# Routed gate and up products of a macaron block (MoE, time mixing, MoE): tokens stationary instead of weights, gated values turned back by transposes

## The chip, the cores and the metric

The kernel runs on one core of one Trainium2 chip. The metric is device time in microseconds, the median over runs; below it stands beside the profile of one execution.

## What is computed

The input x is 16 sequences of 512 tokens with 256 channels, f32. Three residual steps follow each other:

```python
x = x + 0.5 * ffn(layernorm(x))        # "A"
x = x + attn(layernorm(x))             # time mixing, k/v/r products, scan, layernorm, out product
x = x + 0.5 * ffn(layernorm(x))        # "B", same weights as A

def ffn(x):                            # H = 256, I = 128, 8 experts, 2 chosen per token
    shared = (silu(x @ ws_gate.T) * (x @ ws_up.T)) @ ws_down.T      # 256 inner channels
    scores = sigmoid(x @ gate_weight.T); w, idx = top_k(scores, 2); w = 2.5 * w / w.sum()
    y[e] = (silu(x @ w_gate[e].T) * (x @ w_up[e].T)) @ w_down[e].T  # 128 inner channels
    return shared + sum(w[k] * y[idx[k]])
```

## The kernel before

**Stages.** For each feed-forward ("A", then "B") the sequences are taken in four groups each (`SIZES`, L36). For a sequence: LayerNorm; the rows are split into a high and a low f16 half (`row_hi`, `row_lo`), turned by DMA into `xt` (channels on partitions, tokens along); shared products from `xt`; a router; the rank of every token within its expert; and a scatter of the rows by indirect DMA (POOL) into a DRAM buffer `xs` ordered by expert. For a group: a table says which expert each block of 128 slots belongs to. `fetch` (L737) brings blocks of `xs` by a transposing DMA into `xq`, four blocks at a time, a *quad*; the routed products run over quads; results go to DRAM (`y_store`), from where POOL gathers two rows for each token and DVE adds them (`combine`). Between A and B stands the time mixing of the sequence.

**Routed products before.** `gate_up` (L877, part "E" from L900): the table's values are loaded into registers of TensorE (L904) and the addresses of the block's weights are worked out ahead (L911). For the gate (b = 0) and then the up (b = 1) half, for each block j of the quad and each k of two halves of the channels there are three f16 products of 128 x 128 x 128 (L922, L924, L926): high weights with high rows, high weights with low rows, low weights with high rows. The weights are the stationary operand (read through a register address), the tokens move, so the result has inner channels on partitions and 128 tokens along: one PSUM bank holds the gate of four blocks, a second the up. ACT takes silu of the gate bank into `hid` (L1129, `silu`), DVE multiplies by the up bank (L1227, `gated`), and `hid` is at once in the right orientation to be the stationary operand of `down` (L962, f32, the expert's 128 x 256 down weights moving; one product shows as two instructions in the profile). ACT copies the two banks of `down` to `y_sb` (L1146, `evac`).

**Shared products.** L893 to L895 (512 tokens move), gating as above, then a split of `hid` (`hidden_hi`, `hidden_lo`) and f16 products of 256 columns with tokens stationary (L954, L956, L958).

**Other products.** k, v and r projections (L1029), transposes by TensorE of f32 tiles (L1019 before the mixing, L1049 after the scan), the out product (L1063), router (L976, L979).

**Order.** Every engine's instruction list is written by a planner (`Plan`, L64, and `schedule`, L233). Each task has an engine, a cost in us and an urgency; the planner runs the program in its own model and gives each engine the most urgent task that is ready and for which a buffer is free. The urgencies are sums of a due time and a lag: `LATER` by kind, `T_LATER`, `A_LATER`, `B_LATER` by sequence, `G_LATER` by group. PSUM is six banks for everything and two for `down`. `gate_up` of up to four quads may run ahead of their `down` (`AHEAD`), `hid` has four buffers, `xq` four. The engines then run their lists in order, with semaphore waits.

Of the kernel before, what the change touches and what calls it, by code (L numbers as in the profile page):

```python
# [13 lines left out]
P = 128  # L14
# [39 lines left out]
GATE_0, UP_0, GATE_1, UP_1, DOWN = range(5)  # L54
# [18 lines left out]
class Plan:  # L73
# [10 lines left out]
    SHARED = ("hidden_hi", "hidden_lo")  # L84
# [36 lines left out]
    def run(self, takes, frees, follows):  # L121
# [22 lines left out]
        while events:  # L144
# [13 lines left out]
            for e in order:  # L158
# [3 lines left out]
                for k in ready[e]:  # L162
# [3 lines left out]
                    if stream and stream[1] is not None:  # L166
# [3 lines left out]
                        if k[0] in self.SHARED:  # L170
                            n = sum(other[0] == "S" for other in list(turn[stream[0]])[:n])
                        if line.get((k[0], stream[0]), 0) != n:
                            continue
# [59 lines left out]
def schedule():  # L233
    plan = Plan()

    LATER = {"bias": -6.3, "bonus": -53.3, "choose": 17.5, "combine": 1.0, "downE": -14.8, "evac": 17.4, "fetchA": 2.5, "fetchB": 36.2, "gate_upE": 1.8, "gate_upS": 0.6, "gatedE": 8.2, "gatedS": 2.6, "gatherA": 3.5, "gatherB": -15.9, "hidden_hi": 2.6, "hidden_lo": 1.8, "k_copy": 19.6, "k_proj": -61.7, "kv": -17.5, "mix": -0.2, "norm1": -1.5, "norm2": -60.6, "norm3": 50.1, "out_proj": 0.1, "out_resid": -15.2, "part": -65.4, "places": -10.6, "r_proj": -18.8, "rank": -8.4, "receive": -16.5, "resid": 18.2, "route_exp": -8.2, "router": -2.2, "row_hi": 1.3, "row_lo": -12.8, "rstd": -23.6, "rstd_o": -39.0, "scan": -16.6, "scan_turn": 1.3, "scatter": 2.1, "siluE": -15.7, "siluS": 42.3, "stats1": -8.4, "stats2": -6.8, "stats3": 10.4, "stats_o": 14.3, "store": -27.3, "table": -28.2, "table_out": 25.9, "table_turn": -23.3, "tails": -18.3, "top2": -10.7, "total": -0.9, "turn2": -4.9, "turn_rows": -21.3, "v_proj": -29.1, "weights": 0.9, "y_places": 77.9, "y_store": 15.0}
    T_LATER = (-3.2, 0.2, 12.0, -1.8, 3.6, 4.1, 2.4, 5.3, 12.6, -3.2, -4.1, -4.2, -6.1, -13.4, -5.3, -22.0)
    A_LATER = (-3.4, 0.4, -11.1, -2.1, -14.2, -14.7, -19.1, -15.8, -19.6, -17.4, -24.0, -17.7, -21.2, -21.2, -28.9, -11.5)
    B_LATER = (7.4, 15.7, -12.7, -4.0, 9.8, 4.4, 2.8, 10.9, 23.2, 48.0, 74.2, 65.5, 17.7, 54.6, 24.9, 30.2)
    G_LATER = (-3.0, -4.9, -0.1, 11.8, -23.7, 20.7, -21.9, 25.5)  # L240
# [148 lines left out]
    for g in GROUPS["B"]:  # L389
# [3 lines left out]
            "total": 1, "table_turn": 1, "o_bias": 1, "o_mean": 1, "gate_up": 2}  # L393
# [16 lines left out]
    def frees(k):  # L410
# [9 lines left out]
        if name == "silu":  # L420
            gone(("gate_up", key), "bank", 0)
        elif name == "gated":
            gone(("gate_up", key), "bank", 1)
        elif name == "mix":
# [31 lines left out]
    def follows(k):  # L456
# [8 lines left out]
        if name in ("silu", "gated", "hidden_hi", "hidden_lo", "down"):  # L465
# [8 lines left out]
def program(nc, x, w_chunks, w_attn, w_router, channels, consts_in, xs, ys, out):  # L474
# [26 lines left out]
    with ExitStack() as ctx:  # L501
# [3 lines left out]
        def sem(name):  # L505
# [6 lines left out]
        w_hi = [sb(f"w_hi{p}", [P, NCH * P], F16) for p in range(DOWN)]  # L512
        w_lo = [sb(f"w_lo{p}", [P, NCH * P], F16) for p in range(DOWN)]

        wd = sb("wd", [P, 2, NE * P])
# [14 lines left out]
        w_stage = acc[:, NSEQ // 2:, :, :].rearrange("p s j c -> p (s j c)")[:, 0:NCH * GU]\  # L530
            .rearrange("p (c u n) -> p c u n", c=NCH, u=4)
# [91 lines left out]
        silu_done, gated_done = sem("silu_done"), sem("gated_done")  # L623
        hi_done, lo_done = sem("hi_done"), sem("lo_done")
# [33 lines left out]
        def released(name, key, b):  # L658

            if name == "gate_up":  # L660
                return (silu_done, gated_done)[b], chunk_no[key] + 1
            if name == "down":
# [28 lines left out]
        def slots_of(what, f, *which):  # L691
            return T if what == "S" else blocks_of(f, *which) * P

# [10 lines left out]
        def _(sp):  # L704
# [62 lines left out]
            def load_w(i):  # L767
# [5 lines left out]
                for c in range(*SPLITS[i]):  # L773
                    sp.dma_start(w_stage[:, c].rearrange("p u n -> p (u n)"), w_chunks[c][:, 0:GU]).then_inc(w_in[i], 16)
                    to = wd[:, :, c * P:(c + 1) * P] if c < NE else ws_stage[:, :, (c - NE) * P:(c - NE + 1) * P]
                    sp.dma_start(to, w_chunks[c][:, GU:CW].rearrange("p (h n) -> p h n", h=2)).then_inc(wd_in[i], 16)
# [93 lines left out]
        def _(pe):  # L870
# [9 lines left out]
            def gate_up(what, f, *which):  # L880
                key = (what, f, *which)
                if what == "S":
# [5 lines left out]
                    cols = slice((NE + c) * P, (NE + c + 1) * P)  # L888
                    for b, done in ((0, gate_done), (1, up_done)):
                        bank = bank_free("gate_up", key, b)  # L890
# [681 lines left out]
```

## Time and profile before

| | us |
|---|---|
| median of 3 runs | 1129.08 (1127.78 to 1136.01) |
| span of the profiled execution | 1279.5 |
| what lies around the span | not recorded; no separate time of that execution was kept |
| PE busy in the profiled execution | 991.1 (77%) |
| DVE, POOL, ACT busy | 788.2, 695.5, 412.1 |

The profiled execution's span is 150 us longer than the median of the plain runs. Busy times of PE are modelled and overlap, so the spacing of matmuls is read from their starts. PE is the matmuls, PEld the weight loads, PEldq and PEq TensorE's sequencer, L12 a line of the kernel.

### The profile page before, as it was taken

Reading aid. Unit: us, or ns where it says so; the run is one execution under the profiler, and the core shown is the slowest. Engines: PE = TensorE matmul, PEld = TensorE weight load, DVE = VectorE, ACT = ScalarE, POOL = GpSimd, SP = SyncE. Lnnn points to the kernel's source line nnn. Section 1 sums busy time; section 2 is a strip of 40 time slices with the busy share of each in tenths; the row PEclk is TensorE's granted clock in tenths of the full one; section 3 lists DMA queues with packets and bytes.
Section 4 is the critical chain, followed back from the end, with each engine's and each line's share of the span. In section 5 each row is a group of like instructions: output and inputs, shape, how many; then the busy total and the mean of one; then the engine's idle time right before and its main releaser. Section 6 shows DMA issues by size and latency. Waiting matters only on the chain.

```text
span 1279.5 us, 23262 instructions
## 1 busy us (share of the span) xinstructions
PE 991.1 (77%) x7488; PEld 696.8 (54%) x7488; DVE 788.2 (62%) x2485; ACT 412.1 (32%) x737; POOL 695.5 (54%) x684
## 2 busy tenths in 40 slices
PE   2767986889957876989867899778787997877560
PEld 1434663565835544657755576456465675656450
DVE  5855554979655875875247697554587885324233
ACT  5332441445313532423213354112233533212110
POOL 2766445764156885274256334754667455355555
PEclk9888988999979887999878899888988999878875
DMA  8668689673266632337777535764876346679974
GB/s 241 203 182 165 131 217 201 141 177 105 66 150 140 152 99 87 79 103 188 170 166 179 132 83 106 175 188 134 208 154 164 94 92 185 163 184 246 225 194 139
DMA packets 337989, 198.58 MB, mean 155 GB/s; under 512 B 251728, under 2 KB 319952, under 8 KB 337872
## 3 DMA queue, kind: packets, MB, share of 16 engines
q1 hardware_dynamic: 312432, 129.84, 41.8%
q0 software_dynamic: 24576, 67.14, 20.6%
q8 instruction: 64, 1.05, 0.4%
q14 instruction: 53, 0.43, 0.1%
q10 hardware_dynamic: 864, 0.12, 0.1%
HBM read 47.05 MB, written 92.27 MB: 109 GB/s over the span
## 4 chain that ended last, share of the span: by engine, by line
PE 51%; issue 18%; DVE 11%; another core or an unknown queue 7%; POOL 6%; DMA 3%; ACT 2%; SPq 1%; ACTq 0%; POOLq 0%; DVEq 0%
PE ps L1029 11%; PE ps L962 10%; PE ps L922 5%; PE ps L924 5%; PE ps L926 5%; PE ps L1063 3%; PE ps L895 2%; PE ps L893 2%; PE ps L894 2%; POOL xsB L835 2%; DVE acc L1254 2%; PE ps L954 1%; POOL y_got L852 1%; PE ps L958 1%
## 5 line engine op out<-in xcount | busy, mean ns | idle before, releaser
L922 PE MATMUL ps<-xq,w_hi 128*128 128x128 f16 x1248 | 238.2, 231 | 45.2 <-issue 37.8
L926 PE MATMUL ps<-xq,w_lo 128*128 128x128 f16 x1248 | 239.1, 231 | 35.7 <-issue 35.6
L924 PE MATMUL ps<-xq,w_hi 128*128 128x128 f16 x1248 | 238.9, 231 | 29.5 <-issue 29.2
L1227 DVE SCALAR_TENSOR_TENSOR hid<-ps,hid 128x512 f32<-128x512 f32 x144 | 97.2, 678 | 220.2 <-remote 112.3
L962 PE MATMUL ps<-wd,hid 128*128 x624 | 175.1, 425 | 33.2 <-ACT y_sb L1146 11.2
L1129 ACT ACTIVATE hid<-ps 128x512 f32<-128x512 f32 x144 | 85.1, 591 | 328.1 <-remote 185.2
L852 POOL DMA_INDIRECT y_got<-ysB,y_pos x128 | 124.9, 975 | 99.3 <-DVE acc L1254 50.4
L835 POOL DMA_INDIRECT xsB<-rows,pos x128 | 131.6, 1028 | 79.3 <-DVE pos L1384 43.1
L835 POOL DMA_INDIRECT xsA<-rows,pos x128 | 132.1, 1032 | 74.2 <-DVE pos L1384 38.8
L1254 DVE SCALAR_TENSOR_TENSOR acc<-y_got,share,acc 128x256 f32<-128x256 f32 x256 | 127.8, 507 | 58.3 <-DMA y_got<-ysB,y_pos 31.2
L962 PEld LDWEIGHTS ps<-wd,hid 128*128 128x128 f32 x624 | 128.0, 213 | 65.4 <-issue 47.2
L922 PEld LDWEIGHTS ps<-xq,w_hi 128*128 x1248 | 129.2, 104 | 57.8 <-issue 50.4
L852 POOL DMA_INDIRECT y_got<-ysA,y_pos x128 | 130.1, 1016 | 51.1 <-issue 35.8
L924 PEld LDWEIGHTS ps<-xq,w_hi 128*128 x1248 | 129.3, 104 | 43.6 <-issue 40.1
L926 PEld LDWEIGHTS ps<-xq,w_lo 128*128 x1248 | 129.6, 104 | 40.9 <-issue 40.7
L1146 ACT COPY y_sb<-ps 128x512 f32<-128x512 f32 (+1 forms) x160 | 84.2, 581 | 177.6 <-PE ps L962 122.4
L809 POOL TENSOR_TENSOR rstd<-var_eps,neg_half 128x4 f32<-128x4 f32 x48 | 52.2, 1088 | 109.9 <-DVE less_mean L1278 93.4
L893 PE MATMUL ps<-xt,w_hi 128*128 128x512 f16 x256 | 102.9, 402 | 11.1 <-ACT hid L1129 6.2
L895 PE MATMUL ps<-xt,w_lo 128*128 128x512 f16 x256 | 102.3, 400 | 1.9 <-issue 1.9
L894 PE MATMUL ps<-xt,w_hi 128*128 128x512 f16 x256 | 102.6, 401 | 0.3 <-issue 0.2
L826 POOL TENSOR_TENSOR p_exp<-inv_e,best 128x8 f32<-128x8 f32 x32 | 53.9, 1686 | 83.3 <-DVE best L1319 80.6
L954 PE MATMUL ps<-ws_hi,hid_h 128*128 128x256 f16 x256 | 75.0, 293 | 28.5 <-DVE hid_l L1234 19.9
(138 smaller groups left out, 1804.4 us busy)
## 6 DMA issues: line engine op xcount, KB each, us to landing
ysA<-y_sb SPq DMA_DIRECT2D x36, 512.0 KB
ysB<-y_sb SPq DMA_DIRECT2D x36, 512.0 KB
acc<-in_x_dram SPq DMA_DIRECT2D x16, 512.0 KB
out_dram<-acc SPq DMA_DIRECT2D x16, 512.0 KB
xsA<-zeros SPq DMA_DIRECT2D x36, 128.0 KB
xsB<-zeros SPq DMA_DIRECT2D x36, 128.0 KB
acc<-in_w_chunks_dram SPq DMA_DIRECT2D x10, 256.0 KB, 4.7
xq<-xsA SPq DMA_TRANSPOSE x156
```

The lines of the kernel that those rows point to most:

```text
L835: g.indirect_dma_start(out=xs[f, group_of(f, s)], out_offset=bass.IndirectOffsetOnAxis(ap=pos[:, n % N_ROWS, j, k:k + 1], axis=0), in_=row ...
L852: g.indirect_dma_start(out=y_got[:, h, k, :], out_offset=None, in_=ys[f, g_no], in_offset=bass.IndirectOffsetOnAxis(ap=y_pos[:, s, h, k:k ...
L893: nc.tensor.matmul(ps[:, bank, :], w_hi[2 * k + b][:, cols], hi, start=(k == 0), stop=False)
L894: nc.tensor.matmul(ps[:, bank, :], w_hi[2 * k + b][:, cols], lo, start=False, stop=False)
L895: mm = nc.tensor.matmul(ps[:, bank, :], w_lo[2 * k + b][:, cols], hi, start=False, stop=(k == KC - 1))
L922: nc.tensor.matmul(half, w_hi[2 * k + b][:, cols], hi, start=(j == 0 and k == 0), stop=False, skip_group_check=True)
L924: nc.tensor.matmul(half, w_hi[2 * k + b][:, cols], lo, start=False, stop=False, skip_group_check=True)
L926: mm = nc.tensor.matmul(half, w_lo[2 * k + b][:, cols], hi, start=False, stop=(j == many - 1 and k == KC - 1), skip_group_check=True)
L962: mm = nc.tensor.matmul(half, hid[:, b, tok], wd[:, :, cols], start=(j % 2 == 0), stop=(j % 2 == 1 or j == many - 1), skip_group_check=True)
L1029: mm = nc.tensor.matmul(ps[:, bank, :], a32[:, "kvr".index(w), k, m * P:(m + 1) * P], mixed[w][:, k, :], start=(k == 0), stop=(k == KC - 1))
L1227: v.scalar_tensor_tensor(out=hid[:, i % N_HID, some], in0=ps[:, bank_of("gate_up", key, 1), some], scalar=W_UNSCALE, in1=hid[:, i % N_HID, ...
L1254: v.scalar_tensor_tensor(out=acc[:, s, h, :], in0=y_got[:, h, k, :], scalar=share[:, s, h, k:k + 1], in1=acc[:, s, h, :], op0=ALU.mult, op ...
```

## The change

In the routed part the tokens become the stationary operand and the weights move. The weights of gate and up of one expert lie side by side (256 columns, `GU2`), so one product yields gate and up of a block: tokens on partitions, 256 columns along. A block takes 6 products of 256 columns instead of 12 of 128. Bank 0 now holds gate and up of the quad's first two blocks, bank 1 those of the other two. `silu` and `gated` work on each bank by itself. The result has tokens on partitions, so it is turned back: `turn` (four f32 transposes on TensorE into one more PSUM bank) and `unturn` (an ACT copy from it into `hid`), before `down`. The down weights of an expert lie in one run. The shared products keep their form; only where their weights lie changes. The table holds the expert's number times 256 instead of 128. All lags and due times of the planner are new: every value of `LATER`, `T_LATER`, `A_LATER`, `B_LATER` and `G_LATER`, and those that stand in the diff.

```diff
-    FIRST_A = 6.9
-    FIRST_T = 111.2
-    A_LEAD = 243.5
+    FIRST_A = 5.5
+    FIRST_T = 111.1
+    A_LEAD = 243.2
...
-    E_LEAD = 33.4
-    B_LAG = 73.4
-    EB_LAG = 59.1
+    E_LEAD = 32.9
+    B_LAG = 74.1
+    EB_LAG = 63.3
...
-    G_LAG = 84.0
+    G_LAG = 63.8
...
-        add("pe", "gate_up", key, 0.725 * blocks_of(f, a, b) if what == "E" else 2.75, at, after)
-        add("act", "silu", key, 0.6, at + 1.5, [("gate_up", key)])
-        add("dve", "gated", key, 0.7, at + 2, [("silu", key)])
+        add("pe", "gate_up", key, 0.66 * blocks_of(f, a, b) if what == "E" else 2.75, at, after)
+        add("act", "silu", key, 0.6 if what == "S" else 0.8, at + 1.5, [("gate_up", key)])
+        add("dve", "gated", key, 0.7 if what == "S" else 0.9, at + 2, [("silu", key)])
...
-            add("pe", "down", key, 0.48 * blocks_of(f, a, b), at + 4, [("gated", key)])
+            add("pe", "turn", key, 0.132 * blocks_of(f, a, b), at + 3, [("gated", key)])
+            add("act", "unturn", key, 0.63, at + 3.5, [("turn", key)])
+            add("pe", "down", key, 0.48 * blocks_of(f, a, b), at + 4, [("unturn", key)])
...
                 for j in range(many):
-                    for p in range(DOWN):
+                    for k in range(KC):
                         for w in (w_hi, w_lo):
-                            nc.tensor.lower_ap(w[p][:, bass.ds(first[j], P)], for_matmul_weights=True)
+                            nc.tensor.lower_ap(w[k][:, bass.ds(first[j], GU2)])
...
-                    for j in range(many):
-                        half = ps[:, bank, j * P:(j + 1) * P]
-                        cols = bass.ds(first[j], P)
+                    for j in range(2 * b, min(2 * b + 2, many)):
+                        both = ps[:, bank, (j % 2) * GU2:(j % 2 + 1) * GU2]
+                        cols, tok = bass.ds(first[j], GU2), slice(j * P, (j + 1) * P)
                         for k in range(KC):
-                            hi = xq[:, n % N_XQ, k, j * P:(j + 1) * P]
-                            lo = xq[:, n % N_XQ, KC + k, j * P:(j + 1) * P]
-                            nc.tensor.matmul(half, w_hi[2 * k + b][:, cols], hi, start=(j == 0 and k == 0),
+                            hi, lo = xq[:, n % N_XQ, k, tok], xq[:, n % N_XQ, KC + k, tok]
+                            nc.tensor.matmul(both, hi, w_hi[k][:, cols], start=(j % 2 == 0 and k == 0),
                                              stop=False, skip_group_check=True)
-                            nc.tensor.matmul(half, w_hi[2 * k + b][:, cols], lo, start=False, stop=False,
+                            nc.tensor.matmul(both, hi, w_lo[k][:, cols], start=False, stop=False,
                                              skip_group_check=True)
-                            mm = nc.tensor.matmul(half, w_lo[2 * k + b][:, cols], hi, start=False,
-                                                  stop=(j == many - 1 and k == KC - 1), skip_group_check=True)
+                            mm = nc.tensor.matmul(both, lo, w_hi[k][:, cols], start=False,
+                                                  stop=(k == KC - 1 and j in (2 * b + 1, many - 1)),
+                                                  skip_group_check=True)
                     mm.then_inc(done, 1)
+
+            def turn(*key):
+                i, many = chunk_no[key], blocks_of(*key[1:])
+                pe.wait_ge(gated_done, i + 1)
+                bank = bank_free("turn", key, 0)
+                for j in range(many):
+                    tok = slice(j * P, (j + 1) * P)
+                    mm = nc.tensor.transpose(ps[:, bank, tok], hid[:, i % N_HID, tok], ident[:])
+                mm.then_inc(hid_turned, 1)
...
-                        cols = bass.ds(expert_cols[key][j], P)
-                        mm = nc.tensor.matmul(half, hid[:, b, tok], wd[:, :, cols], start=(j % 2 == 0),
+                        half = ps[:, out[j // 2], (j % 2) * C:(j % 2 + 1) * C]
+                        cols = bass.ds(expert_cols[key][j], C)
+                        mm = nc.tensor.matmul(half, hid[:, b, tok], wd[:, cols], start=(j % 2 == 0),
                                               stop=(j % 2 == 1 or j == many - 1), skip_group_check=True)
...
+                for b, (ready, done) in enumerate(((gate_done, silu_first), (up_done, silu_done))):
+                    act.wait_ge(ready, i + 1)
+                    gate, some = quad_half(key, b, 0)
+                    nc.scalar.activation(some, gate, ACT.Silu, scale=W_UNSCALE).then_inc(done, 1)
+
+            def unturn(*key):
+                i, some = chunk_no[key], slice(0, slots_of(*key))
+                act.wait_ge(hid_turned, quad_no[key[1:]] + 1)
+                nc.scalar.copy(hid[:, i % N_HID, some], ps[:, bank_of("turn", key, 0), some]).then_inc(unturned, 1)
...
+                for b, (ready, n, done) in enumerate(((silu_first, quad_no[key[1:]], gated_first),
+                                                      (silu_done, i, gated_done))):
+                    dve.wait_ge((gate_done, up_done)[b], i + 1)
+                    dve.wait_ge(ready, n + 1)
+                    up, some = quad_half(key, b, 1)
+                    v.scalar_tensor_tensor(out=some, in0=up, scalar=W_UNSCALE, in1=some, op0=ALU.mult,
+                                           op1=ALU.mult).then_inc(done, 1)
```

`quad_half` picks, of bank b, the gate (side 0) or up (side 1) columns of its two blocks, and the place in `hid` for them. Both `gate_up` banks of a quad are given back by `gated`, the bank of `turn` by `unturn`.

## Rows read from the trace of the kernel before

**Rows 1.** The page: busy us (share) x instructions; granted clock in 40 slices.
```profile
span 1279.5 us, 23262 instructions
...
PE 991.1 (77%) x7488; PEld 696.8 (54%) x7488; DVE 788.2 (62%) x2485; ACT 412.1 (32%) x737; POOL 695.5 (54%) x684
...
PEclk9888988999979887999878899888988999878875
```

**Rows 2.** The page: the chain that ended last, by engine.
```profile
PE 51%; issue 18%; DVE 11%; another core or an unknown queue 7%; POOL 6%; DMA 3%; ACT 2%; SPq 1%; ACTq 0%; POOLq 0%; DVEq 0%
```

**Rows 3.** Windows: start:end, length, busy PE PEld DVE ACT POOL, clock, DMA, GB/s.
```profile
100.00:1080.00 980.00, 818.23 (x6045) 572.15 (x6044) 656.87 (x2045) 339.27 (x605) 542.71 (x518) 0.91 0.60 143
...
1080.00:1280.00 200.00, 117.75 (x1052) 93.82 (x1049) 63.24 (x157) 32.41 (x61) 97.56 (x102) 0.78 0.74 191
```

**Rows 4.** TensorE's waits: us in total, times, longest us.
```profile
PE ps L922 <- issue: 37.8, 58, 2.7
...
PE ps L926 <- issue: 35.6, 41, 1.9
...
PE ps L924 <- issue: 29.2, 38, 3.3
...
PE ps L962 <- DVE hid L1227: 10.8, 2, 8.7
...
PE ps L954 <- issue: 8.4, 7, 3.1
...
PE ps L958 <- issue: 2.5, 3, 1.1
...
PE ps L956 <- issue: 1.8, 3, 1.1
```

**Rows 5.** The chain in order of time: start us, us, what.
```profile
291.54 1.73 PE ps L962 x8
...
640.01 0.06 PE ps L924
...
643.29 3.29 issue
...
656.06 0.11 PE ps L922
```

**Rows 6.** The timeline: start us, us, engine, line, operation, count.
```profile
619.84 0.27 PE L954 MATMUL ps<-ws_hi,hid_h 128*128 128x256 f16 x1
...
621.04 0.27 PE L958 MATMUL ps<-ws_lo,hid_h 128*128 128x256 f16 x1
...
621.15 0.22 PE L922 MATMUL ps<-xq,w_hi 128*128 128x128 f16 x1
...
623.77 0.22 PE L926 MATMUL ps<-xq,w_lo 128*128 128x128 f16 x1
...
999.98 1.04 PE L1049 MATMUL ps<-ident,state 128*128 128x128 f32 x8
```

**Rows 7.** Three single lines: duration ns min/median/max.
```profile
L904 PEldq TENSOR_LOAD <-tabA x40: 327/334/2647, 90.9 to 887.5; - x40
...
L1049 PE MATMUL ps<-ident,state x128: 269/273/421, 260.8 to 1049.4; 128*128 128x128 f32 x128
...
L911 PEldq FUSED_REGOPS  x472: 51/74/84, 91.5 to 1234.6; - x158
```

**Rows 8.** Groups by shape: busy us, mean ns | idle before, releasers.
```profile
L922 PEld LDWEIGHTS ps<-xq,w_hi 128*128 x1248 | 129.2, 104 | 57.8 <-issue 50.4 <-DMA xq<-xsB 5.2
...
L1227 DVE SCALAR_TENSOR_TENSOR hid<-ps,hid 128x512 f32<-128x512 f32 x136 | 92.8, 686 | 206.8 <-remote 106.7 <-ACT hid L1129 43.1 <-PE ps L926 41.7
...
L1129 ACT ACTIVATE hid<-ps 128x512 f32<-128x512 f32 x136 | 81.1, 597 | 309.9 <-remote 185.2 <-PE ps L926 55.8 <-PE ps L895 50.1
...
L1489 DVE SCALAR_TENSOR_TENSOR acc<-ps,rstdo,acc 128x256 f32<-128x256 f32 x64 | 26.6, 476 | 7.6 <-PE ps L1063 4.4 <-POOL rstdo L819 3.2
...
L1146 ACT COPY y_sb<-ps 128x256 f32<-128x256 f32 x8 | 3.0, 378 | 0.0
```

More of the change, by code:

```diff
@@ L51 @@
 AHEAD = 4
-GATE_0, UP_0, GATE_1, UP_1, DOWN = range(5)
+GU2 = 2 * P
 SPLITS = ((NE, NCH), (0, 4), (4, NE))
@@ L82 @@
     WINDOW, FULL, BESIDE = 3.413, 0.75, 0.9
-    SHARED = ("hidden_hi", "hidden_lo")
+    SHARED, ROUTED = ("hidden_hi", "hidden_lo"), ("turn", "unturn")
     RINGS = ("xt", "xq", "rows", "hid", "split", "y")
@@ L171, in run @@
                             n = sum(other[0] == "S" for other in list(turn[stream[0]])[:n])
+                        if k[0] in self.ROUTED:
+                            n = sum(other[0] == "E" for other in list(turn[stream[0]])[:n])
                         if line.get((k[0], stream[0]), 0) != n:
@@ L392, in schedule @@
     uses = {"turn2": 2, "k_proj": 1, "v_proj": 1, "r_proj": 1, "scan_turn": 2, "out_proj": 2, "router": 1, "rank": 1,
[L393 removed]
+            "total": 1, "table_turn": 1, "o_bias": 1, "o_mean": 1, "gate_up": 2, "turn": 1}
     def takes(k):
@@ L420, in frees @@
         if name == "silu":
-            gone(("gate_up", key), "bank", 0)
+            if key[0] == "S":
+                gone(("gate_up", key), "bank", 0)
         elif name == "gated":
+            if key[0] == "E":
+                gone(("gate_up", key), "bank", 0)
             gone(("gate_up", key), "bank", 1)
+        elif name == "unturn":
+            gone(("turn", key), "bank", 0)
         elif name == "mix":
@@ L464, in follows @@
             return "chunks", None, key
-        if name in ("silu", "gated", "hidden_hi", "hidden_lo", "down"):
+        if name in ("silu", "gated", "hidden_hi", "hidden_lo", "turn", "unturn", "down"):
             return "chunks", key
@@ L508, in program @@
         ps = ctx.enter_context(nc.psum_tensor("ps", [P, 8, 512], F32))
-        w_hi = [sb(f"w_hi{p}", [P, NCH * P], F16) for p in range(DOWN)]
-        w_lo = [sb(f"w_lo{p}", [P, NCH * P], F16) for p in range(DOWN)]
-        wd = sb("wd", [P, 2, NE * P])
+        w_hi = [sb(f"w_hi{k}", [P, NCH * GU2], F16) for k in range(KC)]
+        w_lo = [sb(f"w_lo{k}", [P, NCH * GU2], F16) for k in range(KC)]
+        wd = sb("wd", [P, NE * C])
         ws_hi = sb("ws_hi", [P, 2, NSH * P], F16)
@@ L660, in released @@
             if name == "gate_up":
+                if key[0] == "E" and b == 0:
+                    return gated_first, quad_no[key[1:]] + 1
                 return (silu_done, gated_done)[b], chunk_no[key] + 1
+            if name == "turn":
+                return unturned, quad_no[key[1:]] + 1
             if name == "down":
@@ L692, in slots_of, with quad_half @@
             return T if what == "S" else blocks_of(f, *which) * P
+        def quad_half(key, b, side):
+            many = min(2, blocks_of(*key[1:]) - 2 * b)
+            bank, i = bank_of("gate_up", key, b), chunk_no[key]
+            side_by_side = ps[:, bank, 0:many * GU2].rearrange("p (j u n) -> p j u n", j=many, u=2)
+            return (side_by_side[:, :, side, :],
+                    hid[:, i % N_HID, 2 * b * P:(2 * b + many) * P].rearrange("p (j n) -> p j n", j=many))
         def uses(n, buf, of):
@@ L936, in down @@
                 else:
-                    pe.wait_ge(gated_done, i + 1)
+                    pe.wait_ge(unturned, quad_no[(f, *which)] + 1)
                 if what == "E" and which[1] == 0:
@@ L1085, in _ @@
             pe.wait_ge(consts_dma, 16 * 5)
-            do = {"gate_up": gate_up, "down": down, "router": router, "rank": rank, "total": total,
+            do = {"gate_up": gate_up, "turn": turn, "down": down, "router": router, "rank": rank, "total": total,
                   "table_turn": table_turn, "turn2": turn2, "k_proj": k_proj, "v_proj": v_proj, "r_proj": r_proj,
@@ L1108, in split_hi @@
                     act.wait_ge(w_in[i - 1], 16 * (last - first))
-                    for p in range(DOWN):
-                        ins = nc.scalar.activation(w_hi[p][:, first * P:last * P].rearrange("p (c n) -> p c n", n=P),
-                                                   w_stage[:, first:last, p], ACT.Copy, scale=W_SCALE)
+                    for k in range(KC):
+                        ins = nc.scalar.activation(w_hi[k][:, first * GU2:last * GU2]
+                                                   .rearrange("p (c n) -> p c n", n=GU2),
+                                                   w_stage[:, first:last, k], ACT.Copy, scale=W_SCALE)
                     if i == 1:
@@ L1213, in split_lo @@
                     first, last = SPLITS[i - 1]
-                    cols = slice(first * P, last * P)
-                    for p in range(DOWN):
-                        ins = low(w_lo[p][:, cols].rearrange("p (c n) -> p c n", n=P), w_stage[:, first:last, p],
-                                  w_hi[p][:, cols].rearrange("p (c n) -> p c n", n=P))
+                    cols = slice(first * GU2, last * GU2)
+                    for k in range(KC):
+                        ins = low(w_lo[k][:, cols].rearrange("p (c n) -> p c n", n=GU2), w_stage[:, first:last, k],
+                                  w_hi[k][:, cols].rearrange("p (c n) -> p c n", n=GU2))
                     if i == 1:
```

59 lines of the change are left out of this document (33 added, 26 removed).

## Prediction

> **What bounds the kernel now.** I read the page's busy table and slices first, then the chain that ended last, then the windows, then TensorE's waits, and last the single instructions of one quad. The reader is to see five things.
>
> TensorE has the most work: 991.1 us of a span of 1279.5, with the granted clock mostly near full [rows 1]. The chain that ended last is PE for 51% and "issue" for 18%, then DVE for 11%; ACT has 2% [rows 2]. So about 69% of the path is TensorE working, or standing with nothing to wait for.
>
> The kernel has two stretches. From 100 to 1080 us PE is busy 818 of 980 us; in the last 200 us it is busy 118, at a mean clock of 0.78 and a DMA share of 0.74 [rows 3]. There it is not TensorE's work that sets the pace.
>
> TensorE's own longest waits are "issue" ahead of the three routed gate and up products: 37.8 + 35.6 + 29.2 = 102.6 us over 3744 matmuls, 27 ns each. The same kind of wait ahead of the shared down products of 256 columns (L956, L958) is 1.8 + 2.5 us over 512 matmuls, 8 ns each [rows 4]. They come in bursts: where a matmul takes 0.06 us on the chain at 640.01, a piece of issue of 3.29 us stands a few matmuls later in the same quad [rows 5].
>
> The span is 150 us longer than the median of the runs, 1129.08. The chain's issue is 18% of 1279.5, about 228 us. Recording is the only thing known to differ between the two, and waits that scale with the number of recorded instructions are the first candidate. If the 150 us all came out of issue, 78 of 228 would be left, a third (0.34). I use this as the upper share of an issue wait that a plain run also has, and zero as the lower one. Terms of the sum are read at the profiled execution's scale; where they are array time they go onto the median unchanged, where they are issue they are scaled by that share.
>
> **Routed products.** There are 312 blocks of 128 slots (3744 / 12) in 80 quads (40 of A at L904 [rows 7], as many of B). Before, a block costs 12 matmuls of 128 columns. Between the first L922 of the quad at 621.15 and its last L926 at 623.77 there are 47 steps, 55.7 ns each: 0.669 us a block. After, it is 6 matmuls of 256 columns of the same type. The nearest rows are the shared down products: L954 at 619.84 to L958 at 621.04 is 11 steps, 109.1 ns each [rows 6]: 0.655 us. The same columns pass through the array, so only the small cost per matmul is saved: 0.014 x 312 = 4 us. At the low clock level a 128-column step is 0.11 us [rows 5], twice the columns' time at the full level, and there the form gives back nothing. Bounds: 0 and 4 us; I take 4.
>
> The Trainium skill (TensorE: Matmul & The Clock Gate, Back-to-back issue gap) says that in a stream of weight-load and matmul pairs the sustained spacing at 128 columns is about 81 ns, and that the plain column formula counts too little there. By that a block would cost 0.97 us now and the change would be worth about 0.32 x 312 = 99 us of array time, an estimate from that page. The trace disagrees: the pairs here stand 55.7 ns apart with a fresh weight load for each, so the sum goes by the rows; what would follow if loads did bind is a rival below.
>
> **Transposes.** 312 are added, f32, 128 x 128. The kernel has the same form at L1049: eight take 1.04 us and one lasts 0.273, so a step is (1.04 - 0.27) / 7 = 0.110 us [rows 6, 7]. 312 x 0.110 = 34 us at the full level. The mean granted clock of 0.91 in the middle [rows 3] means that some stretches are at the low level (1.2 instead of 2.4 GHz), where a step is twice as long: with one transpose in seven there, an estimate from that mean less its idle part, 39 us. Bounds 34 and 68. The down product keeps its operands' sizes, 1.73 us for eight instructions of four blocks [rows 5]; its weights now lie in one run instead of two pieces; cost 0, bounds -2 and +2. The addresses worked out per block fall from eight to four; that group of PE's register operations is 472 x 74 ns = 35 us of its sequencer [rows 7], mostly behind matmuls already issued; I give it 0, bounds -10 and 0.
>
> Array time: 39 - 4 = +35 us. As 69% of the chain is PE and issue, I put 0.69 x 35 = 24 us on the path; the ends are 0 and 35.
>
> **Issue waits.** At the 8 ns of 256-column products, 1872 of them cost 16 us. Counting L954's 8.4 us too [rows 4], it is 12.7 / 768 = 17 ns and 31 us. Between them 24, and 3 for the transposes (at L1049 2.6 us for 128): 102.6 - 27 = 76 us less in a profiled execution. On the median I take half of the upper share: 0.17 x 76 = 13 us less; the ends are 0 and 76. The upper end is the case that issue is all real.
>
> **Gating in halves.** Each PSUM bank now holds gate and up of two blocks, so silu and gating are two instructions each. ACT: a 128x256 copy out of PSUM takes 378 ns, the 128x512 silu 597, so +0.16 us a quad; and the new copy of the turned values, which has the silu's size, 0.59: +0.75 x 80 = 60 us of ACT. DVE: a 128x256 operation out of PSUM takes 476 ns, the 128x512 gating 686 [rows 8]: +0.27 x 80 = 21 us. ACT has 2% of the chain and DVE 11% [rows 2]: 1 and 2 us. What hides ACT's 60 is its 32% load [rows 1]; without that cover they cost up to 60.
>
> **The chain of a quad.** Before, after the last up product only the gating (0.69) stands before down. After: silu of the second half 0.38, gating 0.48, four transposes 0.44, copy 0.59: 1.89, so 1.2 us later, plus two more semaphore hops. In the middle other quads and sequences fill that (up to four quads run ahead). It is bare at the end of the last groups: 2 us, bounds 0 and 10. A new wait stands in PE's queue twice: ahead of turn (gated values) and of down (the copy); whatever the new order has put behind them waits too, since one engine's waits are met in the order of its queue. The existing form of this wait, L962 on DVE, is 10.8 us [rows 4]. The turn also takes one of six banks for about 1.1 us a quad, 88 of 6 x 1129 bank-microseconds, 1%: nothing.
>
> **Orders.** All lags are new, and with them SP's and POOL's queues. No instruction of either is added or dropped, and the DMAs have the same sizes (the down weights load as 1 KB runs instead of two of 512 B, once). I give this 0, bounds -15 and +15: no row shows an order that was not run.
>
> **Sum.** 24 - 13 + 2 + 1 + 2 = +16; I round down to +15, as part of the 24 is bound to fall into other engines' waits: 1129 + 15 = 1144 us. For a profiled execution 24 + 5 - 0.69 x 76 = -23: a span near 1256, shorter than before although the plain run is longer.
>
> **Rivals.**
> Issue is real (faster). The bursts of issue [rows 5] hit dense 128-column streams, whatever is recorded, and the change halves their number. For it: the waits per instruction fall from 27 to 8 ns with the wider form [rows 4]. Against it: 150 us of span that plain runs don't have. Price: all of it 24 + 5 - 76 = -47, 1082; a half, -9, 1120. It decides from 29 us of real saving, 38% of the 76, onwards. Chance 0.27, at about 1108.
>
> Loads bind (faster). If a pair held the array for the 104 ns of its weight load [rows 8], a block would take 1.25 us now and 0.655 after, 186 us of array and 0.69 of it on the path: 1129 - 128 + 29 = 1030. The spacing of 55.7 ns speaks against it [rows 6]. Chance 0.02. This is where the rule of 81 ns would lead.
>
> Hidden (no change). PE is idle 162 of the middle's 980 us [rows 3]; if the new order puts turns there, the 35 us cost a third: 1129 + 12 - 13 + 3 = 1131. Chance 0.22.
>
> Waits in order (slower). If half of the 1.2 us longer chain is bare in each quad, 80 x 0.6 = 48 us and 0.69 of it on the path, 33: 1144 + 33 = 1177. For it: one DVE wait at L962 lasted 8.7 us of the 10.8; against it: there were only two. Chance 0.14.
>
> **How the numbers follow.** The forecast has 0.35, with its own range 1132 to 1158 (array on the path 15 to 30, issue 0 to 26, order a few). A measurement of this kernel tells about 1% from no change, 11 us. Faster by over 1% (under 1118): most of the rival with real issue and the 0.02, 0.25. Within 1%: the hidden case, the rest of the first rival and a part of the forecast, 0.32. Slower by over 1% (over 1140): 0.43. Range: 1098 to 1172, which leaves out the ends of the two outer rivals.
>
> **What would show it.** Right: the gate and up group reads x1872 at 256 columns, spaced 0.109; x312 transposes at 0.11; issue ahead of gate and up falls from 103 to 20 to 35 us; span 1235 to 1275. Wrong: a median under 1118 with the span falling by as much as the median (issue was real); L962 or the transposes waiting over 30 us for ACT or DVE (waits in order); gate and up spaced other than 0.109; PE busy outside 100 to 1080 us grown instead of inside.

## The result and the profile after

The changed kernel takes 1158.5 us (median of 4, 1157.4 to 1159.6) against 1131.8 for the kernel before (1127.8 to 1136.0): ratio 1.023, 95% interval 1.020 to 1.027. It is slower, as forecast, by 27 us where +15 was forecast.

The page of the changed kernel: span, busy times, granted clock, and the chain by engine.
```profile
span 1157.4 us, 20370 instructions
...
PE 955.8 (83%) x5928; PEld 667.1 (58%) x5928; DVE 809.1 (70%) x2559; ACT 462.2 (40%) x891; POOL 700.3 (61%) x684
...
PEclk9989999999999989999899999899889999988985
...
POOL 20%; PE 19%; issue 18%; SPq 16%; DVE 12%; DMA 11%; ACT 2%; POOLq 0%; ACTq 0%; DVEq 0%
```
The first surprise is the span: 1157.4, two microseconds from the plain time. The profile read before the prediction was 1279.5, 150 over its plain time, and [rows 1, 2] came from it. So the kernel before was profiled once more, unchanged:

> The kernel before, profiled once more. Theory R (the waits called issue were the recording's): the profiled execution can be anywhere from 1130 to 1280 us, its plain time is 1130, ratio 1.00, and where its span is near 1130 the issue waits ahead of the routed gate and up products are under 15 us instead of 103. Rival (issue is the kernel's own): the span is near 1280 again with about 100 us of issue.

Plain 1132.1 (10 runs), ratio 0.999 (0.997 to 1.002), span of the profiled execution 1130.8. Its page:
```profile
span 1130.8 us, 23262 instructions
...
PE 921.7 (82%) x7488; PEld 667.1 (59%) x7488; DVE 800.4 (71%) x2485; ACT 410.5 (36%) x737; POOL 697.3 (62%) x684
...
PEclk9889999999999989999899899989999999989885
...
PE 23%; POOL 22%; issue 18%; SPq 12%; DVE 11%; DMA 11%; ACT 2%; POOLq 0%; ACTq 0%; DVEq 0%
```
Its waits of TensorE that end in issue, all that the view's first 30 rows have, beside 102.6 us for three lines in [rows 4]:
```profile
PE ps L922 <- issue: 9.8, 15, 1.3
...
PE ps L954 <- issue: 4.2, 3, 2.1
...
PE ps L1063 <- issue: 2.4, 1, 2.4
```
Two things change for the reader. The bursts of [rows 5] belong to the one execution in which they were recorded. And the chain is another one: PE holds 23% of it, not 51%; POOL, SP's queue and DMA hold 45%. The 51% stood on an execution in which TensorE was busy 69 us longer and idle 79 us longer than in the second (991.1 of 1279.5 us against 921.7 of 1130.8); that this made it the late one is my reading. Why that execution was so long is not shown: the second was recorded too. From here on every comparison of profiles is made against this second profile of the kernel before.

What the change does to single instructions is as the prediction had it. The changed kernel's timeline, one quad:
```profile
708.56 0.27 PE L947 MATMUL ps<-w_hi,xq 128*128 x1
...
711.07 0.27 PE L951 MATMUL ps<-w_hi,xq 128*128 x1
```
23 steps in 2.51 us, 109.1 ns each, 0.655 us a block (0.655 predicted). The new transposes, and the halves of silu and gating and the new copy, by line and by group:
```profile
L962 PE MATMUL ps<-ident,hid x312: 272/273/477, 100.4 to 1118.6; 128*128 128x128 f32 x156
```
```profile
L1172 ACT ACTIVATE hid<-ps 128x256 f32<-128x256 f32 x152 | 55.9, 383 | 155.8 <-PE ps L951 147.4 <-PE ps L998 4.3 <-issue 3.1
...
L1283 DVE SCALAR_TENSOR_TENSOR hid<-ps,hid 128x256 f32<-128x256 f32 x152 | 59.1, 418 | 54.1 <-ACT hid L1172 53.9
...
L1177 ACT COPY hid<-ps 128x512 f32<-128x512 f32 x72 | 41.9, 587 | 91.5 <-PE ps L962 81.8 <-issue 9.4
```
383 ns (378 taken), 418 ns (476 taken), 587 ns (590 taken). PE's busy time rises from 921.7 to 955.8, by 34 us; PE's time not busy falls only from 209 to 202 (span less busy). That leaves the question: why was the added work not done in the time in which PE stands? Windows of the kernel before (second profile), then of the changed kernel; columns as in [rows 3]:
```profile
100.00:1000.00 900.00, 796.18 (x6391) 574.00 (x6388) 672.13 (x2054) 344.79 (x619) 554.18 (x531) 0.97 0.69 162
1000.00:1131.00 131.00, 65.14 (x662) 56.76 (x662) 54.20 (x119) 21.56 (x40) 82.22 (x85) 0.79 0.90 237
```
```profile
100.00:1000.00 900.00, 803.28 (x4931) 559.19 (x4928) 674.48 (x2107) 380.47 (x737) 546.70 (x520) 0.97 0.66 157
1000.00:1157.00 157.00, 90.70 (x584) 72.34 (x584) 59.66 (x140) 37.56 (x80) 92.39 (x95) 0.82 0.90 225
```
In the 900 us of the middle PE is busy 7 us longer, and 26 us more of its work is left for the end, which is 26 us longer. Yet 97 us of the middle stay idle. Either the form needs that idle time (its longer chain and its two waits), or the new order does. One sign was on hand before any run: each kernel's planner computes the length of the whole program in its own model (below, the planner's length), and it gives 1068.5 us for the kernel before and 1091.2 for the changed one, 23 us more.

### The profile page after: what moved, and what is told of

Same layout as the page of the kernel before. It is cut to its first block, busy times and chain, and to the rows that moved or that the text cites. A ratio compares the mean times of both kernels' runs of the same rounds, so it can differ in the third digit from the quotient of the medians.

```text
span 1157.4 us, 20370 instructions
## 1 busy us (share of the span) xinstructions
PE 955.8 (83%) x5928; PEld 667.1 (58%) x5928; DVE 809.1 (70%) x2559; ACT 462.2 (40%) x891; POOL 700.3 (61%) x684
## 4 chain that ended last, share of the span: by engine, by line
POOL 20%; PE 19%; issue 18%; SPq 16%; DVE 12%; DMA 11%; ACT 2%; POOLq 0%; ACTq 0%; DVEq 0%
SPq L775 10%; PE ps L1065 6%; POOL y_got L878 6%; POOL xsA L861 5%; DMA y_got<-ysB,y_pos 4%; POOL xsB L861 4%; PE ps L998 3%; DVE acc L1309 2%; PE ps L1099 2%; SPq L748 2%; DMA xq<-xsB 2%; PE ps L947 2%; POOL rstd L835 2%; DMA y_got<-ysA,y_pos 2%; PE ps L949 1%
## 5 line engine op out<-in xcount | busy, mean ns | idle before, releaser
L1309 DVE SCALAR_TENSOR_TENSOR acc<-y_got,share,acc 128x256 f32<-128x256 f32 x256 | 133.5, 523 | 127.2 <-DMA y_got<-ysB,y_pos 75.0
L947 PE MATMUL ps<-w_hi,xq 128*128 x624 | 180.4, 289 | 49.3 <-DMA xq<-xsB 31.3
L949 PE MATMUL ps<-w_lo,xq 128*128 x624 | 180.5, 289 | 0.0
L951 PE MATMUL ps<-w_hi,xq 128*128 x624 | 180.1, 289 | 0.0
L861 POOL DMA_INDIRECT xsA<-rows,pos x128 | 135.2, 1057 | 61.5 <-issue 35.4
L998 PE MATMUL ps<-wd,hid 128*128 x624 | 151.2, 385 | 14.5 <-ACT hid L1177 7.0
L998 PEld LDWEIGHTS ps<-wd,hid 128*128 128x128 f32 x624 | 114.3, 192 | 34.0 <-issue 19.5
L1172 ACT ACTIVATE hid<-ps 128x256 f32<-128x256 f32 (+1 forms) x160 | 58.0, 378 | 157.7 <-PE ps L951 149.2
L947 PEld LDWEIGHTS ps<-w_hi,xq 128*128 128x128 f16 x624 | 64.4, 103 | 71.0 <-DMA xq<-xsB 35.0
L1283 DVE SCALAR_TENSOR_TENSOR hid<-ps,hid 128x256 f32<-128x256 f32 (+1 forms) x160 | 61.0, 411 | 54.9 <-ACT hid L1172 54.6
L1204 ACT ACTIVATE norm<-acc,shift,rstd 128x256 f32<-128x256 f32 x128 | 66.4, 591 | 65.1 <-POOL shift L838 52.0
L1177 ACT COPY hid<-ps 128x512 f32<-128x512 f32 x80 | 45.5, 578 | 92.4 <-PE ps L962 82.7
```

Source lines behind the costliest of these rows:

```text
L861: g.indirect_dma_start(out=xs[f, group_of(f, s)], out_offset=bass.IndirectOffsetOnAxis(ap=pos[:, n % N_ROWS, j, k:k + 1], axis=0), in_=row ...
L947: nc.tensor.matmul(both, hi, w_hi[k][:, cols], start=(j % 2 == 0 and k == 0), stop=False, skip_group_check=True)
L949: nc.tensor.matmul(both, hi, w_lo[k][:, cols], start=False, stop=False, skip_group_check=True)
L951: mm = nc.tensor.matmul(both, lo, w_hi[k][:, cols], start=False, stop=(k == KC - 1 and j in (2 * b + 1, many - 1)), skip_group_check=True)
L998: mm = nc.tensor.matmul(half, hid[:, b, tok], wd[:, cols], start=(j % 2 == 0), stop=(j % 2 == 1 or j == many - 1), skip_group_check=True)
L1309: v.scalar_tensor_tensor(out=acc[:, s, h, :], in0=y_got[:, h, k, :], scalar=share[:, s, h, k:k + 1], in1=acc[:, s, h, :], op0=ALU.mult, op ...
```

## The experiments

All ratios are to the kernel before, measured on the same chip.

**Which half of the change?** The changed kernel under the lags of before:
```diff
-    EB_LAG = 63.3
-    G_LAG = 63.8
+    EB_LAG = 59.1
+    G_LAG = 84.0
...
```


> The changed kernel with the lags and due times of before. Theory A (the added TensorE work is the loss): 1150 to 1185 us, not below the changed kernel's 1158.5. Rival O (the new lags are the loss): 1125 to 1140 us.

1179.5 us, ratio 1.041 (1.036 to 1.047). And the other way round, the old form under the new lags (the same lines exchanged in the kernel before):

> The kernel before with the lags and due times of the changed one. Theory A: the lags were fitted to the other form, so 1130 to 1170 us, no better than before. Rival O (the new lags are bad in themselves): 1155 us or more, as slow as the changed kernel.

1162.2 us, ratio 1.028 (1.023 to 1.033). A's ranges hold for both runs. O's range for the first (1125 to 1140) is missed by 40 us, but its bound for the second holds: a kernel with none of the added work that is as slow as the change. Exchanging lags is no clean cut, because lags fitted to one set of costs are unfitted to another: both mixtures are slower than their own form with its own lags.

**Taking the added work out, order kept.** In the changed kernel:
```diff
             def turn(*key):
-                i, many = chunk_no[key], blocks_of(*key[1:])
-                pe.wait_ge(gated_done, i + 1)
...
+                pass
...
             def unturn(*key):
...
+                pass
...
-                    pe.wait_ge(unturned, quad_no[(f, *which)] + 1)
+                    pe.wait_ge(gated_done, i + 1)
```


> The changed kernel without the transposes and without the copy behind them, order unchanged; down reads the values unturned, so the routed output is another one. Theory A (transposes and copy are the loss, 39 us of array of which most is on the path): 1120 to 1135 us. Rival H (gating in halves and the 256-column products are the loss): above 1150 us.

1148.9 us, ratio 1.018 (1.011 to 1.024): between the ranges of A and H, 14 us above A's. Without the transposes, the copy and their two waits 10 of the 27 us come back by the medians and 6 by the ratios, and the intervals of the two ratios overlap, so it could be nothing. The kernel that is left is busy on TensorE for as long as the kernel before (923.2 and 921.7 us on their pages) and is still 16 us slower than it was on the same chip (1133.2). What it has besides is the halves, the 256-column products, their banks (the first one is now held until its half is gated) and the order.

Where the work was taken out TensorE stands instead, ahead of the routed products and mostly for fetched rows. First the changed kernel, then this one:
```profile
L947 PE MATMUL ps<-w_hi,xq 128*128 x624 | 180.4, 289 | 49.3 <-DMA xq<-xsB 31.3
```
```profile
L946 PE MATMUL ps<-w_hi,xq 128*128 x624 | 181.2, 290 | 78.1 <-DMA xq<-xsB 47.8
```
It waits 29 us longer there, where 33 us of TensorE's busy time are gone.

**Doubling.** The changed kernel with every transpose twice:
```diff
-                for j in range(many):
+                for j in [*range(many), *range(many)]:
                     tok = slice(j * P, (j + 1) * P)
                     mm = nc.tensor.transpose(ps[:, bank, tok], hid[:, i % N_HID, tok], ident[:])
```


> The changed kernel with every transpose made twice, the same order: 312 more at 0.110 us, 34 us of array. Theory P (TensorE's array time goes to the span one for one): 1158.5 + 30 to 38 = 1188 to 1197 us. Rival C (what costs is the longer chain with its two waits, which grows only by 0.44 us a quad, mostly covered): 1160 to 1172 us.

1159.4 us, ratio 1.025 (1.019 to 1.030); the change has 1.023. This is the run that fells theory P, on which my sum rested: 34 us more of array (27 us more of busy time on the page) cost 1 to 2 us, with an interval of about 6 us either way. Its windows show where they went:
```profile
100.00:1000.00 900.00, 823.68 (x5166) 583.81 (x5165) 672.71 (x2104) 381.79 (x735) 545.31 (x519) 0.97 0.67 157
1000.00:1160.00 160.00, 96.59 (x655) 78.76 (x652) 60.21 (x142) 38.30 (x82) 93.11 (x96) 0.85 0.89 222
```
PE is busy 824 us of the middle instead of 803: the doubled transposes stand in time that was idle in the same order.

The copy twice, one after the other:
```diff
+                nc.scalar.copy(hid[:, i % N_HID, some], ps[:, bank_of("turn", key, 0), some]).then_inc(copied, 1)
+                act.wait_ge(copied, quad_no[key[1:]] + 1)
                 nc.scalar.copy(hid[:, i % N_HID, some], ps[:, bank_of("turn", key, 0), some]).then_inc(unturned, 1)
```


> The changed kernel with ACT's copy of the turned values made twice, one after the other: the chain of a quad grows by about 0.7 us and ACT by 50 us, TensorE by nothing. Theory P: 1158 to 1166 us. Rival C: half or more of 80 x 0.7 = 56 us, 1185 us or more.

1160.1 us, ratio 1.026 (1.022 to 1.031): +2 to 3 us against the change, inside P's range. The chain of a quad, longer by a second copy of 0.59 us and the wait between the two, is covered in this order. Rival C (1185 us or more) falls too.

**Single parts in the kernel before.** Silu and gating of a quad in two halves:
```diff
-                some = slice(0, slots_of(*key))
-                nc.scalar.activation(hid[:, i % N_HID, some], ps[:, bank_of("gate_up", key, 0), some], ACT.Silu,
-                                     scale=W_UNSCALE).then_inc(silu_done, 1)
+                for some in halves(key):
+                    ins = nc.scalar.activation(hid[:, i % N_HID, some], ps[:, bank_of("gate_up", key, 0), some],
+                                               ACT.Silu, scale=W_UNSCALE)
+                ins.then_inc(silu_done, 1)
...
```


> The kernel before, its order, with the silu and the gating of a quad as two instructions of half the width each: ACT +13 us, DVE +21 us, TensorE nothing. Theory P: 1132 to 1140 us. Rival D (the work added to DVE is a good part of the loss): 1145 us or more.

1132.5 us, ratio 1.000 (0.997 to 1.003): nothing, and rival D falls. By the pages the halves add 7 us of DVE and 5 of ACT here, not the 21 and 13 expected. And the array time of the transposes alone, in the fitted order of before:
```diff
+                if what == "E":
+                    for j in range(many):
+                        tok = slice(j * P, (j + 1) * P)
+                        nc.tensor.transpose(ps[:, out[0], tok], hid[:, b, tok], ident[:])
```


> The kernel before, its order, with four transposes of the gated values ahead of each routed down product into the bank that this product then overwrites: 34 us of array, no new wait and no copy. Theory P: 1132 + 28 to 38 = 1160 to 1170 us. Rival C (waits, not array time): 1132 to 1145 us.

1140.3 us, ratio 1.009 (1.006 to 1.012): 10 us for 34 (25 by the page's busy time), under P's range and within C's. Array time counts by 0.3 to 0.4 here. The other direction:
```diff
-                            nc.tensor.matmul(half, w_hi[2 * k + b][:, cols], lo, start=False, stop=False,
-                                             skip_group_check=True)
-                            mm = nc.tensor.matmul(half, w_lo[2 * k + b][:, cols], hi, start=False,
+                            mm = nc.tensor.matmul(half, w_hi[2 * k + b][:, cols], lo, start=False,
                                                   stop=(j == many - 1 and k == KC - 1), skip_group_check=True)
```


> The kernel before, its order, with the third of the three routed gate and up products (low weights) left out: 1248 matmuls of 55.7 ns, 69 us of array less. If array time under a fixed order counts one for one: 1062 us. If it counts by a third, as the 34 us of idle transposes did (10 us): 1105 to 1115 us. If the order's waits set all: 1125 to 1132 us.

1123.9 us, ratio 0.993 (0.990 to 0.996): 8 us for 69 (51 by the page's busy time, 921.7 to 870.5), a tenth to a sixth, outside the range for a third and 1 us below that for waits alone. Its windows:
```profile
100.00:1000.00 900.00, 762.00 (x5411) 530.51 (x5409) 678.34 (x2067) 346.07 (x623) 561.71 (x540) 0.95 0.72 165
1000.00:1118.00 118.00, 50.71 (x430) 41.91 (x430) 48.60 (x109) 19.80 (x37) 73.71 (x76) 0.76 0.88 243
```
PE is busy 34 us less in the middle than in the kernel before and simply stands 34 us more there. TensorE is busy for 82% of the span of the kernel before, and still isn't what that kernel waits for most.

**New orders.** No part of the work that was tried accounts for the loss, so the order was next. (The 256-column products and the longer-held bank were not tried by themselves.) A search over the planner's lags, the same for each kernel, gave other orders; in the kernel before, for example, and in the changed one:
```diff
-    EB_LAG = 59.1
-    G_LAG = 84.0
+    EB_LAG = 65.2
+    G_LAG = 52.7
...
-    EB_LAG = 63.3
-    G_LAG = 63.8
+    EB_LAG = 60.0
+    G_LAG = 82.9
...
```
(the other lags differ by similar amounts). The third kernel is that without transposes and copy, and here they are gone from the plan too:
```diff
-            add("pe", "turn", key, 0.132 * blocks_of(f, a, b), at + 3, [("gated", key)])
-            add("act", "unturn", key, 0.63, at + 3.5, [("turn", key)])
-            add("pe", "down", key, 0.48 * blocks_of(f, a, b), at + 4, [("unturn", key)])
+            add("pe", "down", key, 0.48 * blocks_of(f, a, b), at + 4, [("gated", key)])
```

> The kernel before with lags searched anew for it; the planner's own length falls from 1068.5 to 1052.3 (the chip was 61 to 70 us above the planner's length in the four full forms run so far). Theory F (what the order loses or gains on the chip follows the planner): 1112 to 1124 us. Rival N (the planner's gains below its tuned point are noise): 1130 us or more.

> The changed kernel with lags searched anew, as long a search starting from the lags of before; planner's length 1080.7 against 1091.2 of the change. Theory F: 1142 to 1154 us, faster than the change but 25 to 35 us slower than the old form planned again. Rival N: 1155 us or more. Rival U (only the search of the change was unlucky): within 8 us of the old form planned again.

> The new form without transposes and copy, and planned without them (planner's length 1058.8); down reads the values unturned, so the routed output is another one. Theory T (transposes and copy are the form's loss once each kernel has an order of its own): 1120 to 1132 us, 20 us or more below the new form planned again. Rival H (the rest of the form costs as much): above 1138 us.

Measured: 1131.6 us, ratio 0.999 (0.997 to 1.001); 1136.8 us, ratio 1.004 (1.001 to 1.007); 1137.9 us, ratio 1.008 (1.004 to 1.011). The new form with another order is 22 us faster than the change and within half a per cent of the kernel before. The old form gained nothing from 16 us of the planner's length. And the kernel without transposes and copy, with an order of its own, is no faster than the full one: the whole of the added work is worth less than the difference between two orders. Theory F is refuted (its first range missed by 8 us, its second by 5), theory T is missed by 6 us, and U holds for this pair of orders. N holds for the old form and fails by 18 us for the new one; H is at its edge (1137.9 against above 1138).

One order each proves little, so two more for each form were made in the same way, from other starting points. The edit is again the lags only; two of them, for the two new-form kernels and then for the two old-form ones:
```diff
-    EB_LAG = 63.3
-    G_LAG = 63.8
+    EB_LAG = 64.9
+    G_LAG = 53.7
...
+    EB_LAG = 71.5
+    G_LAG = 25.6
...
-    EB_LAG = 59.1
-    G_LAG = 84.0
+    EB_LAG = 53.7
+    G_LAG = 104.6
...
+    EB_LAG = 63.5
+    G_LAG = 32.0
```

> The changed kernel's form with a second order, searched from the lags that were found for the old form (planner's length 1087.3, 4 below that of the change). Theory O (the change's order is an unlucky one among orders that the planner holds equal): anywhere from 1135 to 1165 us. Rival U (the form costs 20 us or more): 1155 us or more.

> As the run before, a third order from another starting point (planner's length 1089.9). Theory O: 1135 to 1165 us. Rival U: 1155 us or more.

> The old form with an order searched from the lags of the new form planned again (planner's length 1061.3, 7 below that of the kernel before). Theory O: 1128 to 1160 us, overlapping the new form's orders. Rival U: 1120 to 1135 us, 20 us below them.

> As the run before, from the starting point of the third order (planner's length 1061.8). Theory O: 1128 to 1160 us. Rival U: 1120 to 1135 us.

Measured, in that order: 1172.5 us, ratio 1.036 (1.031 to 1.042), above the range of O; 1150.9, 1.018 (1.013 to 1.023); 1139.9, 1.007 (1.004 to 1.010); 1139.1, 1.006 (1.003 to 1.009). With the earlier ones:

The windows are those of one profiled execution each; that of the new form planned again took 1131.0 us, the fastest of its ten.

| full kernels | planner's length | PE busy, 100 to 1000 us | PE busy / length of the end | us | ratio |
|---|---|---|---|---|---|
| new form, planned again | 1080.7 | 823 | 64 / 130 | 1136.8 | 1.004 |
| new form, third order | 1089.9 | 815 | 84 / 150 | 1150.9 | 1.018 |
| new form, the change | 1091.2 | 803 | 91 / 157 | 1158.5 | 1.023 |
| new form, second order | 1087.3 | 792 | 102 / 169 | 1172.5 | 1.036 |
| new form, lags of before | 1109.7 | 790 | 111 / 179 | 1179.5 | 1.041 |
| old form, the kernel before | 1068.5 | 796 | 65 / 131 | 1131.8 | 1 |
| old form, planned again | 1052.3 | 800 | 70 / 131 | 1131.6 | 0.999 |
| old form, second order | 1061.3 | 798 | 69 / 139 | 1139.9 | 1.007 |
| old form, third order | 1061.8 | 801 | 70 / 137 | 1139.1 | 1.006 |
| old form, lags of the change | 1103.3 | 790 | 81 / 152 | 1162.2 | 1.028 |

The windows of the best and the worst searched order of the new form:
```profile
100.00:1000.00 900.00, 822.72 (x5102) 578.53 (x5102) 678.67 (x2123) 388.10 (x754) 548.37 (x530) 0.97 0.68 161
1000.00:1130.00 130.00, 63.80 (x400) 50.38 (x400) 52.90 (x128) 27.82 (x60) 82.71 (x85) 0.80 0.92 243
```
```profile
100.00:1000.00 900.00, 792.01 (x4843) 548.93 (x4844) 671.61 (x2103) 378.88 (x730) 535.70 (x514) 0.97 0.64 154
1000.00:1169.00 169.00, 101.97 (x660) 80.59 (x658) 63.19 (x148) 41.41 (x90) 98.48 (x102) 0.80 0.86 224
```
The reader is to see the same pattern in the five rows of the new form. In the last stretch PE stands 66 to 68 us, whatever the order (130 - 64, 150 - 84, 157 - 91, 169 - 102, 179 - 111); in the old form's it is 61 to 71. About 35 us of them lie behind the last down product, where the chain is POOL's gathers, their DMAs and DVE's adds. In the change and in the new form planned again that product is
```profile
1120.20 1.56 PE L998 MATMUL ps<-wd,hid 128*128 x6 [1.30 <-ACT hid L1177]
```
```profile
1092.29 1.56 PE L998 MATMUL ps<-wd,hid 128*128 x6 [1.30 <-ACT hid L1177]
```
and the spans are 1157.4 and 1129.2: 35.6 and 35.4 us behind its end. So the end is as long as these 66 us and the work that is left at 1000 us, and what the order decides is how much of PE's work fits into the middle. The best one does 823 us of it there, with all the added transposes; the change 803.

Does the form cost anything? Over the four searched orders of each form (the change and the kernel before among them), the ratios are 1.004, 1.018, 1.023, 1.036 and 0.999, 1.000, 1.006, 1.007: means 1.020 and 1.003, best against best half a per cent. The sets overlap at one kernel only, and the spread inside the new form, 3.2%, is larger than the change's loss, that inside the old one 0.8%. So neither theory of the last four expectations holds as it was put: the new form can be had for 6 us, but an order found for it in this way costs 19 us more on average than one for the old form, and is more of a lottery. Four orders each fix that average poorly (a standard error of 8 us). The planner's own lengths have a gap of the same kind, 1087.3 and 1061.0 on average, 26 us. They do not rank the orders: the chip is 56 to 85 us above them in these eight, and the new form's worst searched order (1172.5) has its second shortest length.

## Why the prediction was wrong, step by step

**What bounds the kernel: failed, and with it the weight of the array.** "So about 69% of the path is TensorE working, or standing with nothing to wait for" was read from an execution 150 us longer than the plain runs. In the second profile PE is 23% of the chain. From the 69% I put 24 of 35 us of array on the path. At a kept order, 34 us more of array cost 10 us in the kernel before and 1 to 2 in the changed one, and 69 us less gave 8. The term should have been between 1 and 10 us; the rival "hidden" had it about right, at a third of the array, and the sum of 1131 us wrong. A sign of this stood in the prediction as one of being wrong: of the 34 us by which PE's busy time grew, 14 lie between 100 and 1080 us and 20 outside.

**Issue waits: failed in size, the bound held.** I gave back 13 us. The bound "zero as the lower one" is where the truth lies: issue ahead of the routed gate and up products is 9.8 us in the second profile of the kernel before and 4.0 in the changed kernel's, so at most 6 were to be had. The reason given, that 150 us of the span had no counterpart in plain runs, was right; it should have taken the whole term away, and cast doubt on the chain as well. (The 3 us for the transposes were also too small by their own row: 2.6 us for 128 make 6 for 312, which changes the sum by half a microsecond.) The rival "issue is real" fell with it; so did the forecast of a span near 1256.

**Routed products, transposes, halves, copy: right in size.** 0.655 us a block as predicted, 0.273 us a transpose as at L1049, ACT 0.38 and 0.59 as taken, DVE 0.42 instead of 0.48. The 81 ns a pair that the Trainium skill (TensorE: Matmul & The Clock Gate, Back-to-back issue gap) gives for 128 columns is not what these traces show, 55.7 ns; nor do they show the 99 us of array estimated from it. Halves alone cost 0 (ratio 1.000); the forecast had 3 us for them and the copy together.

**The chain of a quad: right.** I gave 2 us. The copy made twice adds 2 to 3 us, and down waits for the new copy only 7 us in all in the changed kernel:
```profile
PE ps L962 <- DVE hid L1283: 16.6, 8, 5.0
...
PE ps L998 <- ACT hid L1177: 7.0, 7, 3.3
```
The rival "waits in order" had as its mark over 30 us of such waits. These two are 24 together, 31 with down's other waits for ACT and DVE (6.3 and 1.0 us), so the mark doesn't decide; the doubled copy does, which was covered.

**Orders: the step that failed most.** "I give this 0, bounds -15 and +15: no row shows an order that was not run." The order of the change costs 22 us against another order of the same work (1158.5 and 1136.8), outside these bounds, and 81% of the loss. That other order is the best of four; against their mean (1154.7) the change's costs 4 us, so most of what the term lacked is not one unlucky order but what this form's searched orders cost on average. The planner's lengths, 1068.5 and 1091.2, had 23 us of it and were in the two kernels when I put the term at nothing. The sign of the forecast was right by luck: a term that was too large (array) stood in for one that I had put at nothing. The kernel without the added work in the change's order, still 1.8% slower than before, is the run that shows it most directly. What makes an order a bad one isn't settled, nor why this form's are worse on average; the runs show where it costs (how much work is left for the end), not by which task, and no single lag was tried by itself.

## What to carry to other kernels

Where a profiled execution is much longer than the plain runs, take a second profile before the chain or any wait is believed. A high busy share does not make an engine's array time count one for one: doubling the suspected work in place, with the order kept, costs one run and tells what it is worth in that order. And where every list is planned, a new form and its new order are two changes: the planner's own lengths are to be read first, and several orders of each have to be compared before the form is judged.

## What the runs showed of the hardware that I had not expected

A profiled execution can be 13% longer than the plain runs of its kernel (1279.5 us of span, granted clock 0.891) and the next one of the same kernel not at all (1130.8, clock 0.941). No run shows whether the recording did it.

Transposes on TensorE did not lower the granted clock. With 34 us more of them at a kept order its mean over the plain runs was 0.943 in the old form (0.937 in the kernel before on the same chip) and 0.947 in the new one (0.939 in the change), steps hardly larger than the spread between executions of one kernel (0.930 to 0.943 in that kernel before). With 69 us of products less it was 0.923 (0.936 before).
